# First tile of the last group's input products moved from GpSimd to VectorE, in a fused convolution and selective-scan kernel

## The chip, the cores and the metric

One core of a Trainium2 chip runs the whole program. The metric is device time in microseconds (us) of one execution, median over runs; lower is better.

## The reference

Layer 0, per image (32 images of 128 channels, 64 x 64 pixels): an attention vector is computed from the image's mean, it builds a 3 x 3 depthwise kernel, the convolution's result goes through two 1 x 1 products, `gelu(y1) * y2`, a norm over the channels, and is added to the input. Layer 1 is a Mamba block over the 4096 pixels as time steps, with 256 inner channels and 16 states each:

```
h = exp(dt_t * A) * h + dt_t * x_t * B_t      # per channel and state
y_t = sum over states of h * C_t
```

then a gate, an output product, a group norm over the image and SiLU, plus the residual. All is float32.

## The kernel before, in words

An image (a batch) is cut into CH = 8 chunks of T = 512 pixels. For a chunk, 256 channels x 16 states = 4096 recurrences are laid over 128 partitions as NT = 32 tiles of 128 x 512: QUADS = 8 groups (quads, q = 0 to 7) of DG = 4 tiles (g = 0 to 3). Quads 0 to 3 belong to the first half of the channels (d = 0), 4 to 7 to the second.

A quad goes through these steps:

- **decay** (ScalarE, line 585): `exp(dt * A)`, one tile into one of three PSUM banks `ps_a`; tile i waits for the scan that used the bank before.
- **input products** `dbx` = `dtx_rep` (dt times x, spread by DMA) times B, the four tiles of a quad in one instruction of 128 x 2048. Even quads: `weigh_inputs` on VectorE (line 810), with B in the PSUM bank `ps_b`, where TensorE puts it by a selection matmul (`select_b`, line 405). Odd quads: `weigh_inputs` on GpSimd (line 925), with B from `b_rep` in SBUF. `dbx` has three slots: slot 0 for even quads, 1 and 2 for the odd ones in turn.
- **scan** (VectorE, line 823): the recurrence, one tile an instruction, 32 a chunk. It writes `hq`, four quads deep.
- **carry** (ScalarE, line 591): the last column of the quad is kept for the next chunk.
- **state products** (GpSimd, line 933): `hq` times C in place, 128 x 2048 a quad, after the carry.
- **sum over the states** (TensorE, line 417) into `ps_acc`, with a first matmul for x times D (line 414) at quads 0 and 4. That first one waits until VectorE has taken the half before out of `ps_acc` (`y_gate`, line 800).

The order is written out by hand. Each engine has a function `chunk` that walks u = 0 to 31; VectorE does scan u and then what is due behind it, the others follow in their own slots. VectorE's input products for the next even quad stand behind scans 5, 13, 21 and 29, so those of the next chunk's quad 0 are made within this chunk. TensorE's selections stand at its slots u = 0, 8, 16 and 24. GpSimd's order in a chunk is: inputs 1, states 7 (of the chunk before), states 0, inputs 3, states 1, states 2, inputs 5, states 3, states 4, inputs 7, states 5, states 6.

Beside the scans VectorE does norm and input addition for the next chunk behind scan 0 (lines 780, 784), `y_gate` behind scans 8 and 24, softplus and dt times x behind scan 16 (lines 789, 793) and a gate behind scan 23 (line 776).

Two chunks of each batch carry more. **Chunk 5** (`ATT_CHUNK`) has the attention of the next image: TensorE's head matmuls in its slot 26, behind the x times D matmul and the sum of quad 4 (lines 313, 314); behind VectorE's scan 27 `att_sums` (line 753 and two more), which waits for them; behind scan 30 `att_weights` (lines 762 to 772), with line 764, a `tensor_scalar` of 128 x 9 from SBUF to SBUF with a scalar per partition. **Chunk 8** (the first of the next image) has the group norm of the image before, and the loop's end. The first chunk runs ahead of the loop, the last seven behind it, without attention.

SyncE issues all DMAs. `spread_dtx` fills a half of `dtx_rep` again once both products' engines have read it (`bmul_dve`, `bmul_pool`).

Of the kernel before, what the change touches and what calls it, by code (L numbers as in the profile page):

```python
# [15 lines left out]
ALU = mybir.AluOpType  # L16
# [4 lines left out]
P = 128  # L21
H = W = 64
L = H * W
T = 512
CH = L // T
# [6 lines left out]
QUADS = SUB // 4  # L32
# [12 lines left out]
NQ = NS // NJ  # L45
DG = 4
DW = P // DG
QUADS = DI * NQ
# [24 lines left out]

POOL_CHUNKS, POOL_SLOTS, ATT_CHUNK = (1, 2, 3, 4), (10, 11), CH - 3
ATT_FC, ATT_H, ATT_MM, ATT_SUM, ATT_EXP, ATT_WTS = 24, 25, 26, 27, 29, 30


def slot(q):

    return 1 + q // 2 % 2 if q % 2 else 0  # L80


def build_program(nc, a, out):
# [7 lines left out]
    with ctx:  # L91
        def sb(name, shape, dt=F32):
            return ctx.enter_context(nc.sbuf_tensor(name, shape, dt))
# [43 lines left out]
        dtx_rep = sb("dtx_rep", [P, DI, DG, T])  # L137
        b_rep = sb("b_rep", [P, 2, NB, T])
        c_rep = sb("c_rep", [P, 2, NQ, T])
        dbx = sb("dbx", [P, 3, DG, T])  # L140
# [8 lines left out]
        ps_b = ctx.enter_context(nc.psum_tensor("ps_b", [P, T], F32))  # L149
# [36 lines left out]
        def _(sp_e):  # L186
# [62 lines left out]
            def spread_dtx(b, c, d):  # L249
                if d == 0:  # L250
                    sp_e.wait_ge(dtx_done, b * CH + c + 1)
                    sp_e.sem_inc(wait_taken, 1)
                    sp_e.dma_start(dtx_d[c % 2].rearrange("d p t -> p d t"), dtx[:]).then_inc(dtx_out, 16)
                    sp_e.wait_ge(dtx_out, 16 * (b * CH + c + 1))
                    sp_e.sem_inc(wait_taken, 1)
                if not (isinstance(b, int) and b * CH + c == 0):
                    sp_e.wait_ge(bmul_dve, (b * CH + c - 1) * (QUADS // 2) + 2 * (d + 1))
                    sp_e.sem_inc(wait_taken, 1)
                    sp_e.wait_ge(bmul_pool, (b * CH + c - 1) * (QUADS // 2) + 2 * (d + 1))
                    sp_e.sem_inc(wait_taken, 1)  # L260
                src = dtx_d[c % 2, d].rearrange("(g w) t -> w g t", g=DG)
                for j in range(NJ):
                    sp_e.dma_start(dtx_rep[DW * j:DW * j + DW, d, :, :], src).then_inc(dtx_repd[d], 16)
# [40 lines left out]
        def _(pe):  # L304
# [68 lines left out]
            def step_dt(b, c):  # L373
                pe.wait_ge(dbl_done, b * CH + c + 1)
                for d in range(DI):
                    last = mm(pp[:, d, :], w["wdt"][:, d * P:(d + 1) * P], dbl[0:NDBL + 1, c % 2, :], start=True, stop=True)  # L376
                last.then_inc(dt_mm, 1)
# [20 lines left out]
                mm(pp[:, 1, 0:2], w["gblock"][:], gst[:], start=True, stop=True).then_inc(gmm_done, 1)  # L398

            def select_b(b, c, q):  # L400
                n = (b * CH + c) * (QUADS // 2) + q // 2
                pe.wait_ge(dbl_done, b * CH + c + 1)
                if not (isinstance(n, int) and n == 0):
                    pe.wait_ge(bmul_dve, n)
                mm(ps_b[:], bsel[:, q % NQ, :], dbl[0:NDBL + 1, c % 2, :], start=True, stop=True).then_inc(bsel_mm, 1)  # L405
# [15 lines left out]
            def chunk(b, c, end):  # L421
                for u in range(NT):
                    s, g = divmod(u, DG)
                    if g == 0 and s % 2 == 0:
                        if s + 2 < QUADS:
                            select_b(b, c, s + 2)
                        elif c + 1 < end:
                            select_b(b, c + 1, 0)
                    if c + 1 < end:
                        for d in range(DI):  # L430
                            if u == PE_XH[d]:
                                step_xh(b, c + 1, d)
                    for d in range(DI):
                        if u == PE_Z[d]:
                            step_z(b, c, d, alone=c + 1 >= end)
                    if g == 2:
                        if s >= 2:
                            sum_states(b, c, s - 2)
                        elif c:
                            sum_states(b, c - 1, s + QUADS - 2)  # L440
                    if c and u == PE_OUT:
                        step_out(b, c - 1, alone=c + 1 >= end)
                    if c + 1 < end:
                        if u == PE_DBL:
                            step_dbl(b, c + 1)
                        if u == PE_DT:
                            step_dt(b, c + 1)
                    if c + 2 < end:
                        for k in range(TAPS):
                            if u == PE_CONV[k]:  # L450
                                step_conv(b, c + 2, k, k + 1)
                        if u == PE_Y:
                            step_y(b, c + 2)
                        if u == PE_GC:
                            step_gc(b, c + 2)
                        if u == PE_VAR:
                            step_var(b, c + 2)
                    if c == CH and u == GN_SUM:
                        group_sums(b)
                    if c == ATT_CHUNK and end > CH:  # L460
                        if u == ATT_FC:
                            pe.wait_ge(o_done, b * CH + c)
                            att_hidden(b + 1)
                        if u == ATT_MM:
                            att_heads(b + 1)
# [30 lines left out]
        def _(act):  # L496
# [50 lines left out]
            def evac_dbl(b, c):  # L547
                act.wait_ge(dbl_mm, b * CH + c + 1)
                if not (isinstance(b, int) and b * CH + c < 2):
                    act.wait_ge(bc_out, 16 * (b * CH + c - 1))  # L550
                    act.wait_ge(bsel_mm, (b * CH + c - 1) * (QUADS // 2))
                A(dbl[0:NDBL, c % 2, :], pp[0:NDBL, 0, :], ACT.Copy).then_inc(dbl_done, 1)  # L552

            def softplus_tail(b, c, k):
# [168 lines left out]
        def _(dve):  # L723
            v = nc.vector
# [76 lines left out]

            def weigh_inputs(b, c, q):
                d = q // NQ
                dve.wait_ge(bsel_mm, (b * CH + c) * (QUADS // 2) + q // 2 + 1)
                if q % NQ == 0:
                    dve.wait_ge(dtx_repd[d], 16 * NJ * (b * CH + c + 1))
                n = (b * CH + c) * QUADS + q
                if not (isinstance(n, int) and n < 2):
                    dve.wait_ge(scan_done, DG * (n - 1))
                v.tensor_tensor(dbx[:, slot(q), :, :], dtx_rep[:, d, :, :],  # L810
                                ps_b[:].unsqueeze(1).to_broadcast([P, DG, T]), ALU.mult).then_inc(bmul_dve, 1)

            def scan(b, c, i):
                q, g = divmod(i, DG)
                m = (b * CH + c) * QUADS + q
                if g == 0:
                    dve.wait_ge(bmul_pool if q % 2 else bmul_dve, (b * CH + c) * (QUADS // 2) + q // 2 + 1)
                    if not (isinstance(m, int) and m < HQ):
                        dve.wait_ge(sum_done, m - HQ + 1)
                    if c % CH:  # L820
                        dve.wait_ge(carry_done, m - QUADS + 1)
                dve.wait_ge(exp_done, (b * CH + c) * NT + i + 1)
                v.tensor_tensor_scan(hq[:, q % HQ, g, :], ps_a[:, i % RA, :], dbx[:, slot(q), g, :],  # L823
                                     carry[:, q, g:g + 1] if c % CH else 0.0, ALU.mult, ALU.add).then_inc(scan_done, 1)
# [25 lines left out]
            def chunk(b, c, end):  # L850
                for u in range(NT):
                    s, g = divmod(u, DG)
                    scan(b, c, u)
                    if g == 1 and s % 2:
                        if s + 1 < QUADS:
                            weigh_inputs(b, c, s + 1)
                        elif c + 1 < end:
                            weigh_inputs(b, c + 1, 0)
# [54 lines left out]
        def _(pool):  # L913
            g = nc.gpsimd

            def weigh_inputs(b, c, q):
                n = (b * CH + c) * QUADS + q
                d = q // NQ
                if q == 1:
                    pool.wait_ge(bc_repd[c % 2], 16 * 2 * NJ * (b * (CH // 2) + c // 2 + 1))  # L920
                if q % NQ == 1:
                    pool.wait_ge(dtx_repd[d], 16 * NJ * (b * CH + c + 1))
                if not (isinstance(n, int) and n < 4):
                    pool.wait_ge(scan_done, DG * (n - 3))  # L924
                g.tensor_tensor(dbx[:, slot(q), :, :], dtx_rep[:, d, :, :],  # L925
                                b_rep[:, c % 2, q % NQ // 2, :].unsqueeze(1).to_broadcast([P, DG, T]),
                                ALU.mult).then_inc(bmul_pool, 1)

            def weigh_states(b, c, q):
# [85 lines left out]
```

## Time and profile before

| | |
|---|---|
| median of 3 runs | 14398.5 us (14397.29 to 14399.63) |
| profiled execution, its own time | 14398.59 us |
| its span, first to last instruction | 14396.8 us |
| busy: GpSimd (POOL) | 13786.2 us, 96% |
| busy: VectorE (DVE) | 13717.4 us, 95% |
| busy: TensorE (PE) | 11107.7 us, 77% |
| busy: ScalarE (ACT) | 10283.7 us, 71% |
| DMA queue q1 | 57.1% of 16 engines |
| chain that ended last | POOL 62%, "issue" 36%, DVE 1% |
| mean granted TensorE clock | 0.851 |

Two engines are near full, and the mean says nothing of which one holds the other in a given chunk; that is read from stretches of the trace. Instructions of an engine overlap a little at their ends, so an instruction's price within a row of them is the distance between two starts, a little under its duration.

### The profile page before, as it was taken

The numbers are of one execution on the slowest core, as the hardware profiler recorded it, in microseconds if no ns is written. First come the engines' busy times: TensorE is split into PE (matmuls) and PEld (weight loads), VectorE is DVE, ScalarE is ACT, GpSimd is POOL, SyncE is SP. The second block draws the span as 40 slices with busy tenths as digits, with TensorE's granted clock in tenths as the row PEclk, the third lists the DMA queues.
The fourth block names the chain that finished last, engine by engine and source line by source line (L and its number), as shares of the span: only waits on it lengthen the run. The fifth ranks groups of instructions, "written<-read, shape, count | busy, mean of one in ns | idle before, by whom it ended". The sixth has DMA issues, their size and how long they took to land.

```text
span 14396.8 us, 149878 instructions
## 1 busy us (share of the span) xinstructions
PE 11107.7 (77%) x32512; PEld 3277.9 (23%) x32512; DVE 13717.4 (95%) x11828; ACT 10283.7 (71%) x17320; POOL 13786.2 (96%) x3076
## 2 busy tenths in 40 slices
PE   6778777777777777778777777777787777777777
PEld 2222222222222222222222222222222222222221
DVE  6999999999999999999999999999999999999999
ACT  5777777777777777777777777777777777777776
POOL 6999999999999999999999999999999999999999
PEclk8888888888888888888888888888888888888887
DMA  5555555555655555555556555655555555656554
GB/s 122 139 137 139 139 144 140 134 141 137 148 135 139 136 141 141 141 141 134 142 140 144 133 141 135 147 137 139 141 135 143 139 142 133 143 135 148 136 138 114
DMA packets 1068196, 1991.53 MB, mean 138 GB/s; under 512 B 123649, under 2 KB 124730, under 8 KB 1067066
## 3 DMA queue, kind: packets, MB, share of 16 engines
q1 hardware_dynamic: 1067066, 1979.43, 57.1%
q8 instruction: 347, 5.69, 0.2%
q14 instruction: 783, 6.41, 0.2%
HBM read 1626.62 MB, written 352.32 MB: 137 GB/s over the span
## 4 chain that ended last, share of the span: by engine, by line
POOL 62%; issue 36%; DVE 1%; POOLq 0%; ACT 0%; PE 0%; SPq 0%; DMA 0%; DVEq 0%; ACTq 0%
POOL hq L933 45%; POOL dbx L925 17%; DVE hq L823 0%; POOLq L932 0%; SPq L196 0%; DVE dbx L810 0%; POOLq L924 0%; ACT pp L604 0%; DVE o L848 0%; PE pp L361 0%; PE pp L325 0%; SPq L190 0%; DMA dtx_d<-sp 0%; PE pp L362 0%; ACT ps_a L585 0%
## 5 line engine op out<-in xcount | busy, mean ns | idle before, releaser
L933 POOL TENSOR_TENSOR hq<-hq,c_rep 128x2048 f32<-128x2048 f32 x2048 | 9246.4, 4538 | 471.6 <-ACT carry L591 471.4
L823 DVE TENSOR_TENSOR_SCAN hq<-ps_a,carry,dbx 128x512 f32<-128x512 f32 x7168 | 8655.1, 1264 | 271.0 <-ACT carry L591 97.4
L585 ACT ACTIVATE ps_a<-dt_rep,A_neg 128x512 f32<-128x512 f32 x8192 | 5569.7, 686 | 3582.7 <-DVE hq L823 3542.3
L925 POOL TENSOR_TENSOR dbx<-dtx_rep,b_rep 128x2048 f32<-128x2048 f32 x1024 | 4637.4, 4529 | 117.8 <-DMA dtx_rep<-dtx_d 117.8
L417 PE MATMUL ps_acc<-hq,dsum 128*32 128x512 f32 x16384 | 2408.3, 663 | 628.4 <-POOL hq L933 628.4
L810 DVE TENSOR_TENSOR dbx<-dtx_rep,ps_b 128x2048 f32<-128x2048 f32 x1024 | 2315.6, 2261 | 17.1 <-DMA dtx_rep<-dtx_d 17.1
L325 PE MATMUL pp<-xin,diag 128*128 128x504 f32 (+3 forms) x4608 | 2213.5, 608 | 6.0 <-ACT diag L617 6.0
L405 PE MATMUL ps_b<-dbl,bsel 41*128 41x512 f32 x2048 | 1296.5, 716 | 400.5 <-issue 215.0
L361 PE MATMUL pp<-x,W_taps 128*128 128x512 f32 x768 | 677.4, 980 | 947.8 <-DVE x L784 665.6
L823 DVE TENSOR_TENSOR_SCAN hq<-ps_a,dbx 128x512 f32<-128x512 f32 x1024 | 1188.3, 1206 | 48.8 <-ACT ps_a L585 30.0
L325 PEld LDWEIGHTS pp<-xin,diag 128*128 128x128 f32 x4608 | 793.1, 189 | 1398.1 <-issue 1398.1
L417 PEld LDWEIGHTS ps_acc<-hq,dsum 128*32 128x32 f32 x16384 | 335.5, 112 | 2413.4 <-issue 1322.3
L414 PE MATMUL ps_acc<-xh,D_diag 128*128 128x512 f32 x1024 | 762.9, 837 | 60.9 <-DVE y L800 57.8
L348 PE MATMUL pp<-gbuf,w_center 128*128 128x512 f32 x512 | 407.2, 887 | 442.3 <-DVE gbuf L776 442.3
L393 PE MATMUL pp<-y,w_Wout 128*128 128x512 f32 x1024 | 505.1, 616 | 255.5 <-ACT dt L612 254.6
L405 PEld LDWEIGHTS ps_b<-dbl,bsel 41*128 41x128 f32 x2048 | 330.0, 201 | 1337.1 <-issue 771.7
L384 PE MATMUL pp<-x,Wz 128*128 128x512 f32 x768 | 433.0, 647 | 178.2 <-ACT xh L545 178.1
L362 PE MATMUL pp<-x,W_taps 128*128 128x512 f32 x768 | 557.3, 819 | 0.0
L361 PEld LDWEIGHTS pp<-x,W_taps 128*128 128x128 f32 x768 | 215.1, 310 | 1389.3 <-DVE x L784 870.4
L376 PE MATMUL pp<-dbl,w_wdt 41*128 41x512 f32 x1024 | 507.0, 615 | 0.7 <-ACT dbl L552 0.7
L370 PE MATMUL pp<-xh,w_Wx 128*40 128x512 f32 x1024 | 490.3, 601 | 1.6 <-ACT sz L569 0.8
L559 ACT ACTIVATE sp<-pp 128x1024 f32<-128x1024 f32 x256 | 262.2, 1024 | 278.0 <-PE pp L376 278.0
(117 smaller groups left out, 10164.2 us busy)
## 6 DMA issues: line engine op xcount, KB each, us to landing
dt_rep<-dt_d SPq DMA_DIRECT2D x2048, 256.0 KB, 5.7
dtx_rep<-dtx_d SPq DMA_DIRECT2D x2048, 256.0 KB, 4.9
c_rep<-bc_d SPq DMA_DIRECT2D x1024, 256.0 KB, 5.4
b_rep<-bc_d SPq DMA_DIRECT2D x1024, 128.0 KB, 2.9
dt_d<-dt SPq DMA_DIRECT2D x256, 512.0 KB, 6.0
dtx_d<-sp SPq DMA_DIRECT2D x256, 512.0 KB, 2.8
out<-o SPq DMA_DIRECT2D x128, 512.0 KB, 3.9
xin<-in_x SPq DMA_DIRECT2D x192, 320.0 KB, 8.7
```

Source lines behind the costliest of these rows:

```text
L325: last = mm(acc[:, ra:rb, ca:cb], diag[:, taps[n], :], rows[:, ra + kh:rb + kh, ca + kw - 1:cb + kw - 1], start=(n == 0), stop=(n == TAPS ...
L361: mm(pp[:, d, :], W_taps[:, 1, d * P:(d + 1) * P], x1_cols(c), start=True, stop=False)
L362: mm(pp[:, d, :], W_taps[:, 0, d * P:(d + 1) * P], x1_cols(c, shift=1), start=False, stop=True).then_inc(xh_mm, 1)
L376: last = mm(pp[:, d, :], w["wdt"][:, d * P:(d + 1) * P], dbl[0:NDBL + 1, c % 2, :], start=True, stop=True)
L405: mm(ps_b[:], bsel[:, q % NQ, :], dbl[0:NDBL + 1, c % 2, :], start=True, stop=True).then_inc(bsel_mm, 1)
L414: mm(ps_acc[:], D_diag[:, d, :], xh[:, c % 2, d, :], start=True, stop=False, skip_group_check=True)
L417: last = mm(ps_acc[DW * g:DW * g + DW, :], dsum[:], hq[:, q % HQ, g, :], start=False, stop=(q % NQ == NQ - 1), skip_group_check=True)
L585: A(ps_a[:, i % RA, :], dt_rep[:, q // NQ, g, :], ACT.Exp, scale=A_neg[:, q // NQ, q % NQ, g:g + 1]).then_inc(exp_done, 1)
L810: v.tensor_tensor(dbx[:, slot(q), :, :], dtx_rep[:, d, :, :], ps_b[:].unsqueeze(1).to_broadcast([P, DG, T]), ALU.mult).then_inc(bmul_dve, 1)
L823: v.tensor_tensor_scan(hq[:, q % HQ, g, :], ps_a[:, i % RA, :], dbx[:, slot(q), g, :], carry[:, q, g:g + 1] if c % CH else 0.0, ALU.mult, ...
L925: g.tensor_tensor(dbx[:, slot(q), :, :], dtx_rep[:, d, :, :], b_rep[:, c % 2, q % NQ // 2, :].unsqueeze(1).to_broadcast([P, DG, T]), ALU.m ...
L933: g.tensor_tensor(quad, quad, c_rep[:, c % 2, q % NQ, :].unsqueeze(1).to_broadcast([P, DG, T]), ALU.mult).then_inc(cmul_done, 1)
```

## The change

The input products of quad 7 are split. VectorE makes the first tile (128 x 512) behind scan 25, with B selected into `ps_b` by a fifth selection matmul; GpSimd makes the other three (128 x 1536) where it made all four. TensorE's slot 24 now selects B for quad 7, and the selection for the next chunk's quad 0 moves from slot 24 to slot 26, where it waits for VectorE's new product. The scans of quad 7 wait for both products, and the counts of `bmul_dve` and `bsel_mm` go by five a chunk.

```
+BY_DVE = (0, 2, 4, 6, 7)
+ND, SHARED, SPLIT = len(BY_DVE), 7, 1
...
             def select_b(b, c, q):
-                n = (b * CH + c) * (QUADS // 2) + q // 2
+                n = (b * CH + c) * ND + BY_DVE.index(q)
...
                     if g == 0 and s % 2 == 0:
-                        if s + 2 < QUADS:
-                            select_b(b, c, s + 2)
-                        elif c + 1 < end:
-                            select_b(b, c + 1, 0)
+                        select_b(b, c, s + 2 if s + 2 < QUADS else SHARED)
+                    if u == 26 and c + 1 < end:
+                        select_b(b, c + 1, 0)
...
             def weigh_inputs(b, c, q):                       # VectorE
                 d = q // NQ
-                dve.wait_ge(bsel_mm, (b * CH + c) * (QUADS // 2) + q // 2 + 1)
+                dve.wait_ge(bsel_mm, (b * CH + c) * ND + BY_DVE.index(q) + 1)
                 if q % NQ == 0:
                     dve.wait_ge(dtx_repd[d], 16 * NJ * (b * CH + c + 1))
                 n = (b * CH + c) * QUADS + q
-                if not (isinstance(n, int) and n < 2):
+                if q == SHARED:
+                    dve.wait_ge(scan_done, DG * (n - 3))
+                elif not (isinstance(n, int) and n < 2):
                     dve.wait_ge(scan_done, DG * (n - 1))
-                v.tensor_tensor(dbx[:, slot(q), :, :], dtx_rep[:, d, :, :],
-                                ps_b[:].unsqueeze(1).to_broadcast([P, DG, T]), ALU.mult).then_inc(bmul_dve, 1)
+                m = SPLIT if q == SHARED else DG
+                v.tensor_tensor(dbx[:, slot(q), 0:m, :], dtx_rep[:, d, 0:m, :],
+                                ps_b[:].unsqueeze(1).to_broadcast([P, m, T]), ALU.mult).then_inc(bmul_dve, 1)
...
                 if g == 0:
-                    dve.wait_ge(bmul_pool if q % 2 else bmul_dve, (b * CH + c) * (QUADS // 2) + q // 2 + 1)
+                    if q % 2:
+                        dve.wait_ge(bmul_pool, (b * CH + c) * (QUADS // 2) + q // 2 + 1)
+                    if q in BY_DVE:
+                        dve.wait_ge(bmul_dve, (b * CH + c) * ND + BY_DVE.index(q) + 1)
...
                     scan(b, c, u)
+                    if u == 25:
+                        weigh_inputs(b, c, SHARED)
...
-                g.tensor_tensor(dbx[:, slot(q), :, :], dtx_rep[:, d, :, :],
-                                b_rep[:, c % 2, q % NQ // 2, :].unsqueeze(1).to_broadcast([P, DG, T]),
+                m = SPLIT if q == SHARED else 0              # GpSimd
+                g.tensor_tensor(dbx[:, slot(q), m:, :], dtx_rep[:, d, m:, :],
+                                b_rep[:, c % 2, q % NQ // 2, :].unsqueeze(1).to_broadcast([P, DG - m, T]),
                                 ALU.mult).then_inc(bmul_pool, 1)
```

The waits of SyncE (before `dtx_rep` is filled again) and of ScalarE (before `dbl` is written again) change only in their counts.

## Rows read from the trace of the kernel before

**Rows 1.** Between softplus starts: length; busy PE, PEld, DVE, ACT, POOL; PEclk, DMA, GB/s

```profile
6943.92:6996.74 52.82, 43.16 (x129) 12.49 (x127) 52.22 (x45) 39.11 (x68) 52.82 (x12) 0.87 0.62 147
6996.74:7050.58 53.84, 44.18 (x128) 12.88 (x126) 52.36 (x44) 39.11 (x68) 53.84 (x13) 0.87 0.61 146
7050.58:7104.41 53.83, 43.68 (x128) 12.85 (x127) 52.35 (x44) 37.95 (x64) 53.83 (x13) 0.87 0.56 134
7104.41:7165.64 61.23, 45.36 (x132) 13.91 (x132) 57.83 (x55) 41.46 (x80) 56.17 (x14) 0.78 0.49 116
7165.64:7218.10 52.46, 41.29 (x127) 12.19 (x126) 52.12 (x45) 37.77 (x63) 52.46 (x13) 0.90 0.59 137
7218.10:7270.60 52.50, 43.28 (x129) 12.85 (x127) 51.19 (x44) 37.74 (x63) 52.50 (x12) 0.87 0.59 140
7270.60:7337.13 66.53, 44.16 (x129) 13.02 (x128) 57.97 (x59) 49.06 (x80) 56.55 (x14) 0.77 0.56 148
```

**Rows 2.** Timeline of VectorE in chunk 4: start, us, what, idle before it

```profile
7029.11 2.46 DVE L823 TENSOR_TENSOR_SCAN hq<-ps_a,carry,dbx 128x512 f32<-128x512 f32 x2 [0.43 <-POOL dbx L925]
...
7038.14 3.63 DVE L823 TENSOR_TENSOR_SCAN hq<-ps_a,carry,dbx 128x512 f32<-128x512 f32 x3 [0.27 <-ACT ps_a L585]
7042.48 2.46 DVE L823 TENSOR_TENSOR_SCAN hq<-ps_a,carry,dbx 128x512 f32<-128x512 f32 x2 [0.71 <-POOL dbx L925]
...
7065.23 0.66 DVE L800 TENSOR_TENSOR y<-ps_acc,sz 128x512 f32<-128x512 f32 x1
7065.81 6.00 DVE L823 TENSOR_TENSOR_SCAN hq<-ps_a,carry,dbx 128x512 f32<-128x512 f32 x5
```

**Rows 3.** Who waited for whom: us in total, times, longest

```profile
DVE hq L823 <- POOL dbx L925: 103.6, 200, 1.7
```

**Rows 4.** Timeline of GpSimd in chunk 4: inputs 7, then states 5 and 6

```profile
7064.63 4.61 POOL L925 TENSOR_TENSOR dbx<-dtx_rep,b_rep 128x2048 f32<-128x2048 f32 x1
7069.11 9.07 POOL L933 TENSOR_TENSOR hq<-hq,c_rep 128x2048 f32<-128x2048 f32 x2
```

**Rows 5.** Timeline of TensorE in chunk 4, slots 24 to 27

```profile
7061.32 1.12 PE L405 MATMUL ps_b<-dbl,bsel 41*128 41x512 f32 x2
...
7065.95 2.08 PE L414 MATMUL ps_acc<-xh,D_diag 128*128 128x512 f32 x2
...
7069.56 1.12 PE L352 MATMUL pp<-sq,w_ones 128*128 128x512 f32 x2 [0.53 <-ACT sq L534]
```

**Rows 6.** Timeline of ScalarE there: first reader of the variance matmul

```profile
7075.85 0.67 ACT L538 ACTIVATE sq<-pp,eps 128x512 f32<-128x512 f32 x1
```

**Rows 7.** Timeline of VectorE in chunk 5: scans 25 to 27, then the attention

```profile
7119.65 3.62 DVE L823 TENSOR_TENSOR_SCAN hq<-ps_a,carry,dbx 128x512 f32<-128x512 f32 x3
7124.72 0.17 DVE L753 TENSOR_TENSOR att<-pp,w_spke_b 128x13 f32<-128x13 f32 x1 [1.45 <-PE pp L314]
...
7132.71 3.76 DVE L764 TENSOR_SCALAR att<-att 128x9 f32<-128x9 f32 x1
```

**Rows 8.** Timeline of TensorE in chunk 5: slot 26, and a later selection

```profile
7119.79 2.07 PE L414 MATMUL ps_acc<-xh,D_diag 128*128 128x512 f32 x2
7121.79 1.94 PE L417 MATMUL ps_acc<-hq,dsum 128*32 128x512 f32 x8
7123.66 0.58 PE L313 MATMUL pp<-hrep,w_ch_wT 16*128 16x2 f32 x2
...
7130.01 2.07 PE L405 MATMUL ps_b<-dbl,bsel 41*128 41x512 f32 x2 [0.51 <-DVE dbx L810]
```

**Rows 9.** Busy time and granted clock in slot 26 of chunk 5, columns as in rows 1

```profile
7118.00:7128.00 10.00, 8.68 (x24) 2.75 (x28) 8.44 (x11) 5.83 (x16) 10.00 (x4) 0.56 0.87 194
```

**Rows 10.** All 32 of line 764: duration in ns, min/median/max

```profile
L764 DVE TENSOR_SCALAR att<-att x32: 231/3799/5046, 51.0 to 13821.9; 128x9 f32<-128x9 f32 x32
```

**Rows 11.** Timeline of GpSimd in chunk 5: the next chunk's inputs 1, states 7

```profile
7131.87 4.57 POOL L925 TENSOR_TENSOR dbx<-dtx_rep,b_rep 128x2048 f32<-128x2048 f32 x1
7140.48 4.52 POOL L933 TENSOR_TENSOR hq<-hq,c_rep 128x2048 f32<-128x2048 f32 x1 [4.04 <-ACT carry L591]
```

More of the change, by code:

```diff
@@ L256, in spread_dtx @@
                 if not (isinstance(b, int) and b * CH + c == 0):
-                    sp_e.wait_ge(bmul_dve, (b * CH + c - 1) * (QUADS // 2) + 2 * (d + 1))
+                    sp_e.wait_ge(bmul_dve, (b * CH + c - 1) * ND + sum(q // NQ <= d for q in BY_DVE))
                     sp_e.sem_inc(wait_taken, 1)
@@ L550, in evac_dbl @@
                     act.wait_ge(bc_out, 16 * (b * CH + c - 1))
-                    act.wait_ge(bsel_mm, (b * CH + c - 1) * (QUADS // 2))
+                    act.wait_ge(bsel_mm, (b * CH + c - 1) * ND)
                 A(dbl[0:NDBL, c % 2, :], pp[0:NDBL, 0, :], ACT.Copy).then_inc(dbl_done, 1)
```

## The prediction

> **What bounds the kernel now.** The page comes first: GpSimd is 96% busy, VectorE 95%, and the chain that ended last runs through GpSimd. That makes GpSimd look like the bound, and a shorter GpSimd a gain. The second view, busy time in the stretches from one softplus to the next, says it holds for part of a batch only [rows 1]. In two stretches (53.84 and 53.83 us) GpSimd is busy throughout and VectorE is not: there GpSimd sets the pace. In the stretch of 52.46 us VectorE idles for 0.34 us alone; the one behind the next group norm has the same length. There VectorE is the bound, and GpSimd uses up a lead that it got while it waited in the attention or the group norm. The stretch of 52.82 us is the passage from one regime to the other. GpSimd idles 5.1 us in the attention's stretch (61.23 less 56.17) and 10.0 us in the group norm's.
>
> The third view is VectorE's timeline in a stretch of the first kind: it waits 0.43 and 0.71 us for GpSimd's input products, and 0.27 us for ScalarE's decay [rows 2]. Over the run 103.6 us of waits for line 925 are named [rows 3]. The prize is therefore what these waits hold up, not GpSimd's busy time.
>
> **Part by part.** *Added to VectorE:* a product of 128 x 512 with one operand in PSUM and one in SBUF, the form of line 800, whose start lies 0.58 us ahead of the next [rows 2]. There are 256 chunks: 256 x 0.58 = **+148.5 us**, all on VectorE's path. Bounds: 0.58 us by pitch, 0.66 by the duration, which would make it 169. I take the pitch, as nothing behind it needs its result at once: three more scans come before quad 7's.
>
> *Removed from GpSimd:* a quarter of one input product. One takes 4.48 us from start to start [rows 4], so 1.12 us a chunk, between 0 (were the price fixed for the instruction) and 1.12; I take 1.1. GpSimd's chunk becomes 53.84 - 1.1 = 52.7 us, VectorE's 52.46 + 0.58 = 53.04. VectorE is then the bound in every ordinary chunk, and its waits for GpSimd go. Against 52.46 us these waits and their small, unnamed parts are worth, in a batch, 0.36, 1.38 and 1.37 us in the first three stretches; some 0.7 in the sixth (52.50 long, idle 1.31, where the half chunk without carries has a decay wait of its own); and about 0.3 in the group norm's, an estimate between 0 and the 0.43 of rows 2. Together 4.1 us. Thirty middle batches make 123; the first and the last, which stay in GpSimd's regime longer, about eight stretches of 1.37, 11. **-134 us**, where the named waits alone would give 104. So far the two sides nearly cancel.
>
> *The decay wait* of 0.27 us stays: ScalarE's run of SiLUs and table loads starts behind scan 5, so it moves up with the scans.
>
> *TensorE:* the selection for quad 7 takes the place of that for the next quad 0 (start 7061.32 in rows 5) and is ready some 4 us before scan 25 ends. The next quad 0's selection now waits for VectorE's new product; in front of scan 30's product there are then four scans, 4.7 us, against 1.1 us for a selection at the high clock and 2.1 at the low one [rows 5]: hidden. Behind it stand the x times D matmul, the sum of quad 4 and the variance matmul, each about 2.9 us later (to the end of scan 25, the product and the selection). The variance matmul ended at 7070.7 and ScalarE reads it at 7075.85 [rows 5, 6]: hidden in an ordinary chunk. SyncE's second half of `dtx_rep` waits for both products, neither of them later than GpSimd's full one was: nothing.
>
> *The attention's stretch* is the place where this order shows, 31 times. VectorE's `att_sums` waits for the head matmuls, already 1.45 us [rows 7]. These stand behind the x times D matmul and the sum, and now behind the selection too. From the end of the new product (scan 25's start plus 1.18 plus 0.58) TensorE needs, at its low clock of 1.2 GHz, 2.0 for the selection, 2.0, 1.9 and 0.95 for the heads [rows 8], some 6.9 us; VectorE is there after two scans, 2.36 us: a wait of 4.6. At 2.4 GHz throughout, with about half of each, it is 1.4. The granted clock in that stretch was 0.56, so near its low level [rows 9], but rises within a run of matmuls (2.08 us for line 414, 1.12 for 352 behind it in rows 5). I take 3.7: 2.25 more than now.
>
> But what follows gives it back. Line 764 works on 128 x 9 elements, took 0.23 us at its shortest and 3.8 in the median [rows 10], and in chunk 5 it ends at 7136.47, just when GpSimd's input product ends (7131.87 + 4.57) [rows 7, 11]. So it is held by that instruction, and the delay of `att_sums` ahead of it costs nothing before: what comes later starts the hold later. The Trainium skill, page "SBUF — State Buffer", section "Who interferes with whom", says that VectorE and GpSimd share a port pair as an exclusive lock, which blocks the later one for the whole instruction of the other; this trace agrees, with the end times just named.
>
> Afterwards GpSimd finishes that product earlier. Its states 6 can start when ScalarE has kept the carry, about 0.9 us after scan 27 (an estimate: a decay of 0.7 as in rows 6, and the copy behind it), then come 4.48 and 4.48 for the inputs 1 [rows 4]: 2.36 + 0.9 + 9.0 = 12.2 us after the new product's end. Line 764 starts 2.36 + 3.7 + 8.0 (the distance from `att_sums` to it in rows 7) = 14.1 us after it. GpSimd then idles for the carry of quad 7, as it does now for 4.04 us [rows 11], and line 764 costs its 0.23. So the stretch changes by +2.25 - 3.53 = -1.28 us beside the 0.58 already counted: 31 x -1.28 = **-40 us**. Bounds: wait 4.6, -0.4 us each, -12 in all; wait 1.4, where GpSimd's end stops it, about -3.1 each, -96.
>
> *The end:* in the last chunks VectorE has little beside the scans and waits for GpSimd, whose chain gets shorter: two quarters of a product (2.2) and VectorE's two new ones hidden in its waits (1.2, counted above): **-4 us**, rounded up; between 0 and this.
>
> **Sum:** 148.5 - 134 - 40 - 4 = -29.5. The profiled execution's own time is 14398.59, a tenth of a microsecond above the median of the runs: 14398.6 - 29.5 = **14369 us**, 0.2% less. A measurement can tell about 0.2%, 28.8 us, from no change, so the forecast lies on that border.
>
> **The rivals.**
> *A. The same, with TensorE at its high clock in slot 26.* Then -96 replaces -40: 14313. For: the clock rises in a run of matmuls. Against: a granted 0.56 now, and the new order puts one more pause ahead of the selection. Chance 0.15.
> *B, slower: line 764 still meets a GpSimd instruction.* Place: the second attention step. It decides when GpSimd's inputs 1 end later than line 764 starts, against a reserve of 14.1 - 12.2 = 1.9 us. If it is held for a whole instruction each time, +2.25 and at worst a further 0.7 in place of -1.28: 31 x 4.2 = 130 above the forecast, 14499; half of it 14434. For: it is held in nearly every batch now [rows 10]. Against: the reserve. 0.1.
> *C, slower: the wait for the selection or its followers shows in ordinary chunks.* If the variance chain or quad 7's product comes 0.3 us late in each, 256 x 0.3 = 77: 14446. Against: reserves of 2 to 4 us in each. 0.08.
> *D. The three-tile product takes as long as the four-tile one.* Then GpSimd keeps 53.84 us in its stretches, no wait goes, and only VectorE's own stretches pay: about 4 x 0.58 = 2.3 less 1.3 in the attention, 1.0 x 31: 14430. Against: 128 x 2048 products of one price per element are all that the trace has, so it can't be excluded. 0.05.
>
> **How the numbers follow.** The forecast's mechanism gets 0.6, between 14345 and 14398 with the bounds of the attention's wait and the product's price. What is left, 0.02, is for things not thought of. Faster by over 0.2% (below 14370): half of the forecast's share, A, and a little: 0.46. Slower by over 0.2% (above 14427): B, C and half of D: 0.14. Range: 14320 to 14425, which takes in most of A and D and leaves out B and C.
>
> **What the changed profile would show.** Right: all ordinary stretches between softplus starts at 53.0 to 53.1 us, with none of 53.8 or 52.46; no wait of VectorE for line 925; GpSimd waiting for the carry in each chunk, some 0.3 us; the new product 0.58 from start to start; `att_sums` waiting 3 to 4.6 us; line 764 down from 3.8 to 0.23 us; the attention's stretch near 60.5. Wrong: line 764 still at 3 us or more (B); VectorE waiting for TensorE at line 810, or for ScalarE before norm (C); inputs 7 at 4.5 us (D); ordinary stretches above 53.3.

## The result and the profile after

The changed kernel takes 14457.35 us (median of 6 runs, 14452.55 to 14466.73) against 14397.9 for the kernel before on the same chips: ratio 1.0042, 95% interval 1.0029 to 1.0055. It is 59 us slower. Forecast were 14369 us and a range up to 14425. The profiled execution took 14459.34 us.

The stretches between two softplus starts tell most of it, as in [rows 1]. Columns: length; busy PE, PEld, DVE, ACT, POOL; granted clock, DMA, GB/s. The first and second are ordinary stretches, the third is the attention's, the fourth the group norm's.

```profile
696.76:750.95 54.19, 44.17 (x129) 12.14 (x128) 52.86 (x46) 38.34 (x67) 53.93 (x13) 0.87 0.63 145
750.95:804.03 53.08, 46.19 (x131) 13.57 (x130) 52.73 (x45) 39.24 (x67) 51.73 (x13) 0.84 0.62 144
857.08:918.69 61.61, 46.97 (x137) 14.22 (x135) 54.88 (x56) 41.63 (x80) 53.27 (x13) 0.81 0.49 118
1025.32:1092.19 66.87, 45.98 (x133) 13.74 (x132) 58.52 (x60) 49.28 (x80) 53.94 (x13) 0.80 0.58 153
```

Before, ordinary stretches were 52.46 to 53.84 long, according to the engine that set the pace. Now 104 of 160 take 53.05 us, as forecast (53.04). Of the other 56, 55 take 54.1 to 54.3, and that was not forecast; the 56th, the last of the run, takes 53.3. GpSimd did get its relief. The costliest groups, kept apart by shape (count | busy us, mean ns | idle before), first GpSimd's two kinds of input products:

```profile
L937 POOL TENSOR_TENSOR dbx<-dtx_rep,b_rep 128x2048 f32<-128x2048 f32 x768 | 3479.8, 4531 | 115.1 <-DMA dtx_rep<-dtx_d 115.1
L937 POOL TENSOR_TENSOR dbx<-dtx_rep,b_rep 128x1536 f32<-128x1536 f32 x256 | 880.3, 3439 | 0.0
...
L832 DVE TENSOR_TENSOR_SCAN hq<-ps_a,carry,dbx 128x512 f32<-128x512 f32 x7168 | 8653.9, 1262 | 166.8 <-issue 110.0 <-ACT ps_a L588 55.3 <-POOL dbx L937 1.5
```

The three-tile product is 1.1 us shorter, and VectorE's scans wait 1.5 us for GpSimd in the whole run, where it was 103.6 [rows 3]. (The 110.0 us put down to "issue" are not new in the main: before, the scans waited 97.4 us for ScalarE's carry and 14.9 for "issue".)

The attention in chunk 5, VectorE's timeline (compare [rows 7]): start, us, what, idle before.

```profile
873.50 0.66 DVE L816 TENSOR_TENSOR dbx<-dtx_rep,ps_b 128x512 f32<-128x512 f32 x1
874.08 2.45 DVE L832 TENSOR_TENSOR_SCAN hq<-ps_a,carry,dbx 128x512 f32<-128x512 f32 x2
881.15 0.17 DVE L756 TENSOR_TENSOR att<-pp,w_spke_b 128x13 f32<-128x13 f32 x1 [4.62 <-PE pp L318]
...
889.29 0.23 DVE L767 TENSOR_SCALAR att<-att 128x9 f32<-128x9 f32 x1
```

The new product takes 0.58 us from start to start. Then `att_sums` waits 4.62 us, where it was 1.45 in [rows 7]; the means of 31 batches are 4.58 and 0.99. And the 128 x 9 `tensor_scalar` (now line 767) takes 0.23 instead of 3.76. TensorE at that place (compare [rows 8]) runs everything at its lower clock; the granted clock is 0.50 from 872.3 to 881.0, so already ahead of the first row:

```profile
874.21 2.07 PE L409 MATMUL ps_b<-dbl,bsel 41*128 41x512 f32 x2 [1.92 <-DVE dbx L816]
876.22 2.07 PE L418 MATMUL ps_acc<-xh,D_diag 128*128 128x512 f32 x2
878.22 1.94 PE L421 MATMUL ps_acc<-hq,dsum 128*32 128x512 f32 x8
880.09 0.58 PE L317 MATMUL pp<-hrep,w_ch_wT 16*128 16x2 f32 x2
```

A long ordinary stretch, VectorE, the rows that waited:

```profile
738.03 0.69 DVE L803 TENSOR_TENSOR y<-ps_acc,sz 128x512 f32<-128x512 f32 x1 [0.70 <-PE ps_acc L421]
...
750.95 1.23 DVE L792 SCALAR_TENSOR_TENSOR pp<-pp,sp 128x1024 f32<-128x1024 f32 x1 [0.56 <-ACT sp L568]
```

And TensorE in the same stretch: the first and the last two of the four input matmuls (lines 365 and 366), the sum of quad 6, the z matmuls (388), the sum of quad 7 and the `dbl` matmul (374).

```profile
725.78 1.13 PE L365 MATMUL pp<-x,W_taps 128*128 128x512 f32 x2 [2.13 <-DVE x L787]
...
727.60 1.02 PE L365 MATMUL pp<-x,W_taps 128*128 128x512 f32 x2
728.46 1.02 PE L366 MATMUL pp<-x,W_taps 128*128 128x512 f32 x2
729.41 1.06 PE L421 MATMUL ps_acc<-hq,dsum 128*32 128x512 f32 x8
730.41 1.13 PE L388 MATMUL pp<-x,Wz 128*128 128x512 f32 x2
734.39 1.62 PE L388 MATMUL pp<-x,Wz 128*128 128x512 f32 x2 [2.86 <-ACT xh L548]
735.94 1.94 PE L421 MATMUL ps_acc<-hq,dsum 128*32 128x512 f32 x8
737.81 2.14 PE L374 MATMUL pp<-xh,w_Wx 128*40 128x512 f32 x4
```

The granted clock in the same stretch, columns as above: in the block, in the pause, over the second z matmul and over the sum of quad 7.

```profile
725.78:729.41 3.63, 3.63 (x8) 1.43 (x9) 3.63 (x4) 1.54 (x4) 3.63 (x2) 1.00 1.00 260
731.50:734.39 2.89, 0.03 (x1) 0.00 (x1) 2.89 (x3) 2.71 (x4) 2.89 (x1) 1.00 0.00 0
734.39:735.94 1.55, 1.55 (x2) 0.30 (x3) 1.55 (x2) 1.01 (x2) 1.55 (x2) 0.66 0.00 0
735.94:737.81 1.87, 1.87 (x10) 0.20 (x9) 1.39 (x2) 1.75 (x2) 1.87 (x1) 0.50 0.00 0
```

The same place in a stretch of 53.05 us:

```profile
1174.26 1.18 PE L365 MATMUL pp<-x,W_taps 128*128 128x512 f32 x2 [2.79 <-DVE x L787]
1175.23 1.91 PE L366 MATMUL pp<-x,W_taps 128*128 128x512 f32 x2
1176.93 1.86 PE L365 MATMUL pp<-x,W_taps 128*128 128x512 f32 x2
...
1182.87 1.13 PE L388 MATMUL pp<-x,Wz 128*128 128x512 f32 x2 [1.16 <-ACT xh L548]
1183.93 1.06 PE L421 MATMUL ps_acc<-hq,dsum 128*32 128x512 f32 x8
```

The granted clock there is 0.50 in the middle of the block and 1.00 over the second z matmul and the sum:

```profile
1175.23:1178.63 3.40, 3.40 (x5) 1.35 (x4) 3.40 (x4) 2.20 (x4) 3.40 (x1) 0.50 0.66 186
1182.87:1184.92 2.05, 2.05 (x10) 0.45 (x10) 2.05 (x3) 1.88 (x4) 2.05 (x2) 1.00 0.00 0
```

In the long stretch the input matmuls run at the high clock (about 0.9 us apart; 1.7 is the low one), so TensorE is early and pauses 2.86 us for ScalarE's SiLU; its clock is still high in the pause and falls just behind it. The second z matmul takes longer, the sum and `dbl` come late, and VectorE waits twice. In the short stretch two of the four input matmuls are slow, the pause is 1.16 us, and what VectorE needs comes at the high clock. The fast block gains nothing: in both stretches the second z matmul starts 8.61 us after the first input matmul, when ScalarE releases it. Sorted by the time from the first input matmul's start to the last one's end, the ordinary stretches of the changed kernel are (here and below without the run's last one, which takes 53.3 with a fast block):

| block of the four input matmuls | stretches | their length |
|---|---|---|
| 3.7 us (all at the high clock) | 55 | 54.1 to 54.3, all of them |
| 5.1 to 5.6 us | 79 | 53.0 to 53.1, all |
| over 6.3 us | 25 | 53.0 to 53.1, all |

In the kernel before, no ordinary stretch had a block under 5 us. There the granted clock at the block's start was 0.50 in all 160; in the changed kernel it is 1.00 in 106 of them, and in 56 of these it stays so through the block and most of the pause.

So there are two suspects: the attention's chain, 61.58 us in the mean against 60.5 forecast, and TensorE's clock in ordinary stretches, where the excess over 53.05 adds up to 63 us.

### The profile page after: what moved, and what is told of

The parts are those of the page before. It is cut to its first block, busy times and chain, and to the rows that moved or that the text cites. A ratio compares the mean times of both kernels' runs of the same rounds, so it can differ in the third digit from the quotient of the medians.

```text
span 14457.5 us, 153624 instructions
## 1 busy us (share of the span) xinstructions
PE 11542.7 (80%) x33024; PEld 3355.2 (23%) x33024; DVE 13732.8 (95%) x12084; ACT 10253.9 (71%) x17320; POOL 13527.5 (94%) x3076
## 4 chain that ended last, share of the span: by engine, by line
POOL 69%; issue 27%; DVE 1%; PE 1%; ACT 1%; POOLq 0%; SPq 0%; DMA 0%; DVEq 0%; ACTq 0%
POOL hq L945 47%; POOL dbx L937 22%; DVE hq L832 1%; DVE dbx L816 0%; POOLq L944 0%; SPq L200 0%; ACT ps_a L588 0%; PE pp L329 0%; PE pp L365 0%; ACT pp L607 0%; POOLq L935 0%; DVE pp L792 0%; PE ps_acc L421 0%; PE pp L388 0%; DVE o L857 0%
## 5 line engine op out<-in xcount | busy, mean ns | idle before, releaser
L937 POOL TENSOR_TENSOR dbx<-dtx_rep,b_rep 128x2048 f32<-128x2048 f32 (+1 forms) x1024 | 4360.1, 4258 | 115.1 <-DMA dtx_rep<-dtx_d 115.1
L816 DVE TENSOR_TENSOR dbx<-dtx_rep,ps_b 128x2048 f32<-128x2048 f32 (+1 forms) x1280 | 2481.7, 1939 | 15.9 <-DMA dtx_rep<-dtx_d 15.9
L421 PE MATMUL ps_acc<-hq,dsum 128*32 128x512 f32 x16384 | 2474.5, 680 | 23.3 <-POOL hq L945 23.3
L409 PE MATMUL ps_b<-dbl,bsel 41*128 41x512 f32 x2560 | 1687.3, 744 | 735.9 <-DVE dbx L816 658.1
L365 PE MATMUL pp<-x,W_taps 128*128 128x512 f32 x768 | 592.1, 863 | 994.5 <-DVE x L787 530.7
L409 PEld LDWEIGHTS ps_b<-dbl,bsel 41*128 41x128 f32 x2560 | 430.4, 210 | 1849.9 <-DVE dbx L816 1137.4
L418 PE MATMUL ps_acc<-xh,D_diag 128*128 128x512 f32 x1024 | 793.5, 868 | 2.2 <-DVE y L803 2.2
L366 PE MATMUL pp<-x,W_taps 128*128 128x512 f32 x768 | 527.5, 778 | 0.0
```

Of the source, the lines that this page charges most:

```text
L365: mm(pp[:, d, :], W_taps[:, 1, d * P:(d + 1) * P], x1_cols(c), start=True, stop=False)
L366: mm(pp[:, d, :], W_taps[:, 0, d * P:(d + 1) * P], x1_cols(c, shift=1), start=False, stop=True).then_inc(xh_mm, 1)
L418: mm(ps_acc[:], D_diag[:, d, :], xh[:, c % 2, d, :], start=True, stop=False, skip_group_check=True)
L421: last = mm(ps_acc[DW * g:DW * g + DW, :], dsum[:], hq[:, q % HQ, g, :], start=False, stop=(q % NQ == NQ - 1), skip_group_check=True)
L816: v.tensor_tensor(dbx[:, slot(q), 0:m, :], dtx_rep[:, d, 0:m, :], ps_b[:].unsqueeze(1).to_broadcast([P, m, T]), ALU.mult).then_inc(bmul_dv ...
L937: g.tensor_tensor(dbx[:, slot(q), m:, :], dtx_rep[:, d, m:, :], b_rep[:, c % 2, q % NQ // 2, :].unsqueeze(1).to_broadcast([P, DG - m, T]), ...
```

## The experiments

**1. The moved selection, put behind the heads.**

```
-                    if u == 26 and c + 1 < end:
+                    if u == 27 and c + 1 < end:
                         select_b(b, c + 1, 0)
```

> The changed kernel, with the selection for the next chunk's quad 0 in TensorE's slot 27 instead of 26, so behind the sum of quad 4 and, in chunk 5, behind the head matmuls. Theory (the selection's wait in front of the heads is what costs in chunk 5): the wait of VectorE at att_sums falls from 4.62 us to 0.3 to 1.5, the attention's stretch from 61.6 to about 58.5 us, 31 x 3.1 = 95 us off: 14362. If the long ordinary stretches (54.2 us, 55 of them, in place of 53.05) go too, since TensorE's work ends earlier ahead of the first input matmuls and these start at the low clock again as before the change: a further 65 us off, 14297. Rival (the fifth selection loads TensorE wherever it stands): stretches of 54.2 stay as many, att_sums still waits over 3 us, time within 20 us of 14457.

Measured 14303.61 us, ratio to the kernel before 0.9934 (0.9918 to 0.9951), 153.7 us off the changed kernel. Both parts of the theory came true: all 160 ordinary stretches take 53.05 us, and the attention's takes 58.57. The granted clock at the block's start is 0.50 again in all 160.

```profile
642.84:695.89 53.05, 43.78 (x130) 12.92 (x129) 52.70 (x45) 38.80 (x67) 52.26 (x13) 0.87 0.61 146
855.06:913.63 58.57, 44.18 (x137) 13.51 (x135) 56.21 (x57) 41.64 (x80) 53.28 (x13) 0.85 0.51 123
```

`att_sums` waits 0.25 us there, and at most 0.85 in the other batches. The small `tensor_scalar` is partly held again, since VectorE reaches it while GpSimd's product still runs:

```profile
L767 DVE TENSOR_SCALAR att<-att x32: 231/1586/1917, 51.2 to 13734.0; 128x9 f32<-128x9 f32 x32
```

**2. The same in chunk 5 alone**, to separate the two.

```
-                    if u == 26 and c + 1 < end:
+                    if u == (27 if c == ATT_CHUNK else 26) and c + 1 < end:
```

> The changed kernel, with the next quad 0's selection in slot 27 in chunk 5 alone, and in slot 26 elsewhere. It separates the two parts of what e1 gained (153.7 us). Theory: the attention's stretch 58.6 instead of 61.6, 31 x 3.0 = 94 us off; the stretches of 54.2 stay about as many: 14363. If they come from the attention's disturbance of the phase and not from the slot, they go too: 14304.

Measured 14427.9 us, ratio 1.0021 (1.0011 to 1.003). The attention's stretch is 58.58, as in experiment 1: 31 x 3.0 = 93 us. But the long stretches became more: 65 of 160 (excess 77 us), and the first half of chunk 8 joined them with 53.8 instead of 52.4 in 30 of 31 batches, which makes 41 us. So the long ordinary stretches don't follow from the attention's; they need the slot 26 in ordinary chunks. Why there are 65 and not 55 is not shown. All 65 have a block of 3.7 us, and none of the others has.

**3. The second z matmul behind the sum**, alone and with experiment 1.

```
-PE_XH, PE_Z, PE_DBL, PE_DT, PE_OUT = (1, 2), (3, 5), 7, 10, 18
+PE_XH, PE_Z, PE_DBL, PE_DT, PE_OUT = (1, 2), (3, 7), 7, 10, 18
```

> The changed kernel, with the second z matmul in TensorE's slot 7 instead of 5, so that the sum of quad 7 stands ahead of the pause for ScalarE's SiLU and not behind it. Theory (in the long ordinary stretches TensorE pauses 2.9 us for the SiLU, its clock falls, and the z matmul, the sum and what follows come late at the low clock, so that y_gate waits 0.7 us and softplus 0.6): y_gate's wait goes, the pause gets 1 us shorter, most of the 55 stretches of 54.2 us become 53.05: 14457 - 65 = 14392, attention's stretch unchanged at 61.6. Rival (TensorE is late there because of the moved selection in slot 26, not because of the pause): the stretches stay at 54.2, time within 15 us of 14457.

> Both edits together. Theory: all ordinary stretches 53.05, attention's stretch about 58.5, 14457 - 95 - 65 = 14297, faster than the kernel before by 0.7%. If the two causes are one, it gives no more than the better of the two edits alone.

Measured 14538.93 us (1.0099, 1.0083 to 1.0116) and 14429.54 (1.0022, 1.0012 to 1.0031): 82 and 126 us slower than without the edit. `y_gate`'s wait did go, but the edit fails both ways, and neither forecast came true (14392 and 14297). Where the block is slow, the z matmul is 1 us late, ScalarE's second SiLU with it, and the decay for scan 9 comes late: with both edits VectorE's waits for decays are 228.3 us against 88.6 in experiment 1. Where the block is fast, `dbl` gets a pause of its own behind the first one, and the clock stays low for longer. From a stretch of 57.0 us of the edit alone:

```profile
682.60 1.06 PE L421 MATMUL ps_acc<-hq,dsum 128*32 128x512 f32 x8
685.53 1.55 PE L388 MATMUL pp<-x,Wz 128*128 128x512 f32 x2 [1.87 <-ACT xh L548]
687.85 3.61 PE L374 MATMUL pp<-xh,w_Wx 128*40 128x512 f32 x4 [0.78 <-ACT sz L572]
```

The four passes of `dbl` take 3.6 us here and 1.9 at the high clock. Of the 33 stretches with a fast block in the edit alone (the run's last among them), all with this first pause of 1.87 us, 21 are long (55.3 to 57.0), and in just these the clock falls behind it; in the other 12 it stays at 1.00, and they take 53.05. So a shorter pause is not enough by itself, and it is the clock behind it that the length follows. The totals did not tell the clock's theory from its rival, as the edit moved work as well; the group norm's stretches alone pay 35 of the 82 us.

**4. GpSimd's part alone.** The kernel before, with quad 7's product on tiles 1 to 3; tile 0 is left out.

```
+                m = 1 if q == 7 else 0
-                g.tensor_tensor(dbx[:, slot(q), :, :], dtx_rep[:, d, :, :],
+                g.tensor_tensor(dbx[:, slot(q), m:, :], dtx_rep[:, d, m:, :],
...
```

> The kernel before, with GpSimd's product of quad 7 on three tiles and the first tile left out (the scan reads what quad 3's product left there); no new product on VectorE, no new selection. It measures what the relief of GpSimd is worth by itself. By the forecast's term: VectorE's waits for line 925 go, 14398 - 134 - 4 = 14260, with ordinary stretches of 52.46 us; the attention's stretch would shrink in addition by up to 3.5 us (line 764 no longer held), down to 14150. Rival (the waits' removal only uncovers other waits): 14330 or more, with stretches above 52.9.

Measured 14210.93 us, ratio 0.987 (0.9854 to 0.9886): 187.7 us off. Every ordinary stretch is 52.46. The attention's is 59.2 instead of 61.2 (62 us in all), since line 764 is held 1.7 us in the median and not 3.8. The rest is 126 us, for which the forecast had 134 and 4.

**5. The pause filled.** The first z matmul of each chunk made twice, then three times: the same result, written again.

```
+                for _ in range(0 if alone or d else 1):        # 2 in the second kernel
+                    mm(pp[:, 2 - 2 * d, :], Wz[:, d * P:(d + 1) * P], x1_cols(c), start=True, stop=True)
                 mm(pp[:, 2 - 2 * d, :], Wz[:, d * P:(d + 1) * P], x1_cols(c), start=True, stop=True).then_inc(z_mm, 1)
```

> The changed kernel, with the first z matmul of each chunk made twice, so that about 1.05 us of the pause ahead of the second z matmul is work. Theory (the clock falls in that pause when it is near 3 us long): in the chunks where the first matmuls ran at the high clock the pause goes from 2.9 to about 1.8 us, the clock stays high, and the 55 stretches of 54.2 us become 53.05: 65 us off, 14392, although 256 matmuls are added. Rival (those chunks are long because TensorE has too much to do): the added matmuls make them longer or more of them, 14457 or more. A cost of either: where the first matmuls run at the low clock there is no pause to fill, and what follows comes up to 1 us later; that is hidden if it stays under the margin that softplus has.

> As e5_filled_pause, with the first z matmul made three times: 2.1 us of added work behind the input matmuls. To be read by stretch, sorted by how long the block of the four input matmuls took (3.7 us: all of it at the high clock; up to 6.8 us: nearly all at the low one). In the changed kernel all 55 stretches with a block of 3.7 us are long (54.2), with one z matmul more 12 of 42 are. Theory (the pause behind the block costs the clock, and the lower clock behind it costs the stretch): with the pause filled to under 1 us, none of the stretches with a 3.7 us block is 54 us or longer. Those with a longer block get later by the added work and are 53.9 to 55. Rival (a fast block is only a sign of something else that makes the stretch long): they stay long. In sum slower than e5, 14450 to 14550, by either.

Measured 14447.62 us (1.0034, 1.0021 to 1.0047) and 14541.07 (1.0102, 1.0085 to 1.0119). The totals do not tell the theory from its rival (the first missed its 14392). Sorted by block the stretches do:

| | block 3.7 us | of these 54 us or longer | block over 6.3 us |
|---|---|---|---|
| changed kernel | 55 | 55 | 25, at 53.05 |
| one matmul more | 42 | 12 | 32, at 53.7 to 53.9 |
| two more | 64 | 0 | 15, at 54.6 to 54.7 |

With two matmuls in it the pause is 1.1 us and what follows stays at the high clock. The rows below are from a stretch of 53.05 us: the end of the block, the sum of quad 6, the added copies (line 389), the two z matmuls (390), the sum of quad 7 and `dbl`.

```profile
677.27 1.02 PE L366 MATMUL pp<-x,W_taps 128*128 128x512 f32 x2
678.22 1.06 PE L423 MATMUL ps_acc<-hq,dsum 128*32 128x512 f32 x8
679.22 1.99 PE L389 MATMUL pp<-x,Wz 128*128 128x512 f32 x4
681.04 1.02 PE L390 MATMUL pp<-x,Wz 128*128 128x512 f32 x2
683.20 1.13 PE L390 MATMUL pp<-x,Wz 128*128 128x512 f32 x2 [1.14 <-ACT xh L550]
684.26 1.06 PE L423 MATMUL ps_acc<-hq,dsum 128*32 128x512 f32 x8
685.26 1.91 PE L374 MATMUL pp<-xh,w_Wx 128*40 128x512 f32 x4
```

Adding useless work made these stretches shorter, from 54.2 to 53.05, as the theory of pause and clock has it and its rival does not. With one matmul more the pause is 2.00 us in all 42, and the length again goes with the clock and not with the pause: behind it the clock falls in 12, the 12 long ones, and stays at 1.00 in the other 30. Stretches with a slow block paid for the added work, and with two more also the 80 between the classes, at 53.2 to 53.3. In sum the ordinary stretches were still 25 and 20 us shorter than in the changed kernel; the second total is worse because the group norm's stretches cost 51 us more, the attention's 17 and the first half of chunk 8, 21.

**6. The high clock forced**, on the kernel of experiment 1. First the selection for quad 2 made three times, then in addition the variance matmul four times.

```
+                for _ in range(2 if q == 2 else 0):
+                    mm(ps_b[:], bsel[:, q % NQ, :], dbl[0:NDBL + 1, c % 2, :], start=True, stop=True)
...
+                for _ in range(3):
+                    mm(pp[:, 0, :], w["ones"][:], sq[:], start=True, stop=True)
```

> The kernel of e1_sel_after_heads (14303.6 us, all ordinary stretches 53.05), with the selection for quad 2, which stands ahead of a pause of 3.9 us, made three times. The 2.1 us of added work lies in the pause and delays nothing directly. Theory (what decides is the clock at which the input matmuls behind that pause start: low, and TensorE comes to the SiLU's wait late and keeps its clock; high, and it comes early, pauses near 3 us, and loses its clock for the chain to softplus): the input matmuls start at the high clock in many chunks, and stretches of 54 us and above come back: 14303 + 60 to 250. Rival (the clock before does not matter, only what is queued ahead of what): 14303 plus or minus 10.

> The kernel of e1_sel_after_heads (14303.6 us) with the variance matmul made four times and the selection for quad 2 three times: 5.2 us of added work in pauses that nothing reads from for as long, so that TensorE hardly pauses ahead of the input matmuls. e6_pause_before_xh_filled had not brought these to the high clock. Theory (a block at the high clock is followed by a long pause and a fallen clock): blocks of 3.7 us appear, and just those stretches are 54 us or longer: 14303 + 1.1 for each, 30 to 200 of them, 14340 to 14520. Rival (the order of work alone decides): all ordinary stretches stay 53.05 also where the block takes 3.7 us, 14305.

The first measured 14305.22 us (0.9936, 0.9919 to 0.9952), no change. It is no test of the theory, as the edit did not do what it was made for: the granted clock at the block's start stayed 0.50 in all 160 stretches, and no block took under 5.1 us. The second measured 14389.14 us (0.9997, 0.9987 to 1.0006), 85.5 more than experiment 1. Blocks of 3.7 us came back in 34 ordinary stretches, and just these 34 are 54 us or longer (54.1 to 55.5); the other 125 take 53.05. One of them, with the pause and the low clock behind it:

```profile
734.37 1.13 PE L390 MATMUL pp<-x,Wz 128*128 128x512 f32 x2
737.68 2.03 PE L390 MATMUL pp<-x,Wz 128*128 128x512 f32 x2 [2.19 <-ACT xh L552]
739.64 1.80 PE L425 MATMUL ps_acc<-hq,dsum 128*32 128x512 f32 x8
```

This stretch is 1.85 us over 53.05. VectorE's waits in it are 0.98 for that sum, 0.21 for softplus, and 0.55 at norm, which the repeated variance matmuls delayed directly. So about a third of this excess is the edit's own price and no effect of the clock. Such a wait at norm stands in 30 of the 34. The other four have none and still take 54.05, 54.06, 54.07 and 55.53, with 0.8 to 1.15 us of wait for the sum, and the match with the fast blocks has no exception.

## Why the prediction was wrong

- **VectorE's product, +148.5 us: right.** 0.58 us from start to start, and ordinary stretches of 53.05 where 53.04 stood.
- **GpSimd's waits, -134, and the end, -4: right within a tenth.** Experiment 4 gives 126 for both. Experiment 1 is the whole change without its side effects: 94.3 us under the kernel before. The attention's stretch is 2.64 us shorter there with the new product's 0.58 in it, so 3.22 by itself, 31 x 3.22 = 100 us; the other terms leave 5.5 us of loss where the forecast had 10.5. The group norm's stretch is 66.9 us in the mean there, and 66.7 in the kernel before: 0.58 more and 0.3 less was forecast.
- **The attention, -40: mechanism right, a term mis-sized.** The step was "I take 3.7" for `att_sums`' wait. The trace shows 4.62 in 27 of 31 batches and 4.3 in the others, which is the low-clock bound (stated as 4.6; its own terms, 6.85 less 2.36, give 4.5). The prediction let the clock rise within the run of matmuls; it was at 0.50 from before the new pause of 1.9 us to the run's end. That line 767 would be free at 0.23 us was right in all 31. The stretch came to 61.58 instead of 60.5: 33 us.
- **"Hidden in an ordinary chunk": the step that failed.** The 2.9 us delay behind scan 25 was checked against the readers of each matmul in the chain, and each had its margin, so TensorE's part was put at nothing outside the attention. Nothing was asked about what later work does to the pauses that follow it, and to the clock behind them. It cost 63 us, 1.15 in each of 55 stretches. Rival C named ordinary chunks and a price of 77 us, but for another reason (the variance chain or the product itself), and neither of these was late. Its sign, ordinary stretches above 53.3, did appear.
- The two, 33 and 63, less 6 in the group norm's stretches (66.8 us in the mean, 67.0 by the forecast's terms), come to 90; the miss is 88 us.
- Rivals A, B and D fell: the clock was low over the head matmuls, line 767 never met GpSimd, and the three-tile product is 1.1 us shorter.
- Two sums of the prediction don't come out as written. B, C and half of D add up to 0.205, not 0.14. And the range was said to take in most of A and D, whose times, 14313 and 14430, lie just outside it.

Settled by experiments are the shares (1 and 2), the worth of GpSimd's relief (4), and that stretches with a fast block are long by the clock that falls behind the pause in front of the second z matmul (5, with 3 and 6 pointing the same way). Not settled is why slot 26 brings the high clock to the block, and why it lasts through the block in one chunk and not in the next: the 55 and 65 long stretches lie irregularly. In the changed kernel the pause ahead of the block is 2.0 to 2.5 us in the long stretches and 1.8 to 3.4 in the others, so the pause alone does not tell them apart; with the selection in slot 27 it is 2.8 to 3.9 and no block is fast.

The version of experiment 1 beats both kernels: 14303.6 us, 0.66% under the one before.

## What to carry to other kernels

Work moved between two nearly full engines was priced well by splitting the batch into stretches with one bound each. What broke the forecast was the third engine, which had slack everywhere: when an instruction that waits is put into its in-order queue, ask what stands behind it (here the heads; one slot later costs nothing) and where its pauses go. A matmul queue that runs early and then pauses can deliver the next result later than one that was slow throughout.

## What the runs showed of the hardware

- The granted clock of TensorE couples pauses to later work: behind a pause of 2.86 us the sum of 8 matmuls took 1.94 us at a granted 0.50, behind one of 1.14 to 1.16 it took 1.06 at 1.00, for the same shapes. These are the levels of 1.2 and 2.4 GHz. In the stretch shown the clock was still 1.00 in the long pause and fell behind it. A pause's length alone does not decide: behind 2.00 us it fell in 12 of 42 stretches (experiment 5), behind 1.87 in 21 of 33 (experiment 3). The Trainium skill, page "TensorE: Matmul & The Clock Gate", section "Part 1: The HAM clock gate", says that activity releases the throttle and idling brings it back; these rows agree.
- A `tensor_scalar` on 128 x 9 elements took from 0.23 to 5.05 us, by what GpSimd was doing [rows 10]: 3.8 in the median before, 1.6 in experiment 1, and 0.23 in all 32 in the changed kernel. Its time follows from the phase of two engines, and most of a delay ahead of it can be free: in the changed kernel `att_sums` waited 3.6 us longer than before in the mean, and the attention's stretch grew by 0.4, with the new product's 0.58 in it.
